# Second layer's first normalisation: gamma, beta and root applied by VectorE in two passes instead of by GpSimd in three

## The reference

```
# layer 2, end
out = out @ Wo + bo
x = out + hidden_state
mu = jnp.mean(x, axis=-1, keepdims=True)
var = jnp.var(x, axis=-1, keepdims=True)
return (x - mu) * jax.lax.rsqrt(var + EPS) * gamma + beta      # EPS 1e-06
# layer 3, begin
residual = hidden_states
x = layer_norm(hidden_states, ln1_w, ln1_b)                    # eps 1e-05
```

## Time and profile before

| | |
|---|---|
| time, median of 3 runs | 2528.74 us (2528.33 to 2530.09) |
| profiled execution | 2529.28 us |
| its span | 2527.1 us |
| TensorE busy | 2434.0 us, 96% |
| VectorE busy | 1253.2 us, 50% |
| GpSimd busy | 1119.7 us, 44% |
| ScalarE busy | 1096.3 us, 43% |
| mean granted clock of TensorE | 0.988 of 2.4 GHz |

### The profile page before, as it was taken

How to read it: one execution, slowest core, us unless ns; L and a number is a source line. 1 busy time by engine, 2 the same in 40 slices (tenths; PEclk the granted TensorE clock), 3 DMA queues, 4 the chain that set the end, 5 groups by cost and what they waited for, 6 DMA issues and landing times.

```text
span 2527.1 us, 49031 instructions
## 1 busy us (share of the span) xinstructions
PE 2434.0 (96%) x18400; PEld 2041.9 (81%) x18400; DVE 1253.2 (50%) x3744; ACT 1096.3 (43%) x3712; POOL 1119.7 (44%) x1972
## 2 busy tenths in 40 slices
PE   7999999999999999998888999999999999999999
PEld 6888887888888878886777788888888888788887
DVE  5665655323224667766787332233555565432332
ACT  5555654111114787787787111112555555211111
POOL 3444435600053787878797720042345433740000
PEclk9999999999999999998999999999999999999999
DMA  4121212311033223233353420022122111320100
GB/s 156 68 68 59 97 39 84 96 50 51 5 107 128 76 106 122 92 103 125 134 187 121 133 77 19 32 96 68 34 80 64 51 51 51 107 98 1 50 34 17
DMA packets 107866, 198.36 MB, mean 78 GB/s; under 512 B 9392, under 2 KB 36720, under 8 KB 104688
## 3 DMA queue, kind: packets, MB, share of 16 engines
q1 hardware_dynamic: 107632, 195.22, 23.0%
HBM read 136.47 MB, written 58.72 MB: 77 GB/s over the span
## 4 chain that ended last, share of the span: by engine, by line
PE 78%; ACT 9%; DVE 5%; POOL 4%; DMA 2%; issue 1%; SPq 0%; DVEq 0%; POOLq 0%
PE banks L327 69%; PE banks L468 5%; ACT plain_high L746 5%; PE banks L498 3%; ACT plain_low L746 2%; POOL plain_high L1404 2%; DVE plain_low L1034 1%; ACT plain_work L811 1%; POOL plain_low L1404 1%; DVE stats L1164 1%; PE banks L522 1%; ACT plain_work L730 1%; DVE rounded_low L1083 1%; DMA plain_high<-attention_w 0%; DVE plain_high L1034 0%
## 5 line engine op out<-in xcount | busy, mean ns | idle before, releaser
L327 PE MATMUL banks<-rounded_work,rounded_low 128*128 128x512 f32 (+1 forms) x2688 | 522.9, 349 | 11.7 <-DVE rounded_low L1202 9.1
L839 ACT ACTIVATE plain_work<-banks,columns 128x512 f32<-128x512 f32 x192 | 132.4, 690 | 860.9 <-PE banks L327 860.9
L327 PEld LDWEIGHTS banks<-rounded_work,rounded_low 128*128 128x128 f32 x2688 | 434.7, 193 | 76.2 <-issue 12.4
L327 PE MATMUL banks<-rounded_work,rounded_high 128*128 128x512 f32 (+1 forms) x2400 | 483.8, 355 | 1.4 <-DMA rounded_work<-ctx_split 0.9
L327 PEld LDWEIGHTS banks<-rounded_work,rounded_high 128*128 128x128 f32 x2400 | 397.0, 191 | 67.1 <-issue 5.5
L1373 DVE CAST rounded_work<-plain_work 128x512 fp32r<-128x512 f32 x192 | 104.5, 544 | 685.5 <-ACT plain_work L839 675.0
L1404 POOL TENSOR_SCALAR plain_high<-plain_high,inv_sum 128x128 f32<-128x128 f32 (+1 forms) x768 | 297.1, 413 | 303.5 <-DVE inv_sum L1056 303.1
L327 PE MATMUL banks<-rounded_low,rounded_work 128*128 128x512 f32 x1728 | 416.1, 392 | 0.0
L327 PE MATMUL banks<-rounded_high,rounded_work 128*128 128x512 f32 (+1 forms) x1728 | 391.4, 378 | 0.0
L327 PEld LDWEIGHTS banks<-rounded_low,rounded_work 128*128 128x128 f32 x1728 | 321.4, 188 | 70.6 <-issue 4.4
L327 PEld LDWEIGHTS banks<-rounded_high,rounded_work 128*128 128x128 f32 x1728 | 309.0, 188 | 62.5 <-issue 3.0
(11 more groups left out here) (109 smaller groups left out, 3327.9 us busy)
## 6 DMA issues: line engine op xcount, KB each, us to landing
plain_work<-x SPq DMA_DIRECT2D x96, 256.0 KB, 3.0
plain_work<-mlp_w SPq DMA_DIRECT2D x96, 256.0 KB, 2.7
rounded_work<-ctx_split SPq DMA_DIRECT2D x16, 1024.0 KB, 5.7
u<-plain_work SPq DMA_DIRECT2D x48, 256.0 KB, 2.1
plain_work<-u SPq DMA_DIRECT2D x12, 1024.0 KB, 7.1
x<-plain_work SPq DMA_DIRECT2D x48, 256.0 KB, 2.3
plain_work<-attention_w SPq DMA_DIRECT2D x44, 256.0 KB, 2.7
ctx_split<-rounded_work SPq DMA_DIRECT2D x8, 1024.0 KB, 5.6
```

The source lines that it names most:

```text
L327: mm = pe.matmul(dst, lhs(i), rhs(j), start=first and n == 0, stop=last and n == 2, skip_group_check=True)
L839: act.activation(gelu[:, j % 2, :], bank(key), ACT.Gelu_apprx_tanh, bias=col(m.y, 28 + j)).then_inc(evac_of(key), 1)
```

## The change

GpSimd keeps the first two steps of `pool_root` in the second layer, the epsilon and the power. The three passes behind them are dropped there. VectorE gets a new function `dve_unit`, called at the head of `dve_again`: it waits for GpSimd's root, computes (x - mean) * gamma in place in the hidden row, waits for that, and computes that times root plus beta, again in place. The second buffer is then written by `pool_again` alone, so the wait for its last store moves there. The first pass now raises the count `rooted` and the second raises `norm_ready`.

```
+        def dve_unit(dve, y, b):
+            rt = y.root(b)
+            i = rt % 2
+            h = hidden[:, b % 2, :]
+            if b == 0:
+                dve.wait_ge(gb_loaded, 32)
+            dve.wait_ge(rstd_done, rt + 1)
+            dve.scalar_tensor_tensor(out=h, in0=h, scalar=neg_mean[:, i:i + 1], in1=gamma, op0=ALU.add, op1=ALU.mult).then_inc(rooted, 1)
+            dve.wait_ge(rooted, rt + 1)
+            dve.scalar_tensor_tensor(out=h, in0=h, scalar=rstd[:, i:i + 1], in1=beta, op0=ALU.mult, op1=ALU.add).then_inc(norm_ready, 1)
```

```
@@ pool_root
-            u = (unit_g if y.kind == GQA else unit_c)[:, b % 2, :]
-            pool.wait_ge(u_stored[b % 2], stored_count(y.b0 + b - 2))
-            pool.tensor_scalar(u, h, neg_mean[:, i:i + 1], rstd[:, i:i + 1], ALU.add, ALU.mult).then_inc(rooted, 1)
-            if y.kind == GQA:
-                if b == 0:
-                    pool.wait_ge(gb_loaded, 32)
-                pool.wait_ge(rooted, rt + 1)
-                pool.tensor_tensor(u, u, gamma, ALU.mult).then_inc(scaled, 1)
-                pool.wait_ge(scaled, b + 1)
-                pool.tensor_tensor(h, u, beta, ALU.add).then_inc(norm_ready, 1)
@@ pool_again
+            pool.wait_ge(u_stored[b % 2], stored_count(y.b0 + b - 2))
```

More of the change, by code:

```diff
@@ L199, in build @@
         eps_done, rstd_done, rooted = sem("eps_done"), sem("rstd_done"), sem("rooted")
-        scaled, norm_ready = sem("scaled_by_gamma"), sem("norm_ready")
+        norm_ready = sem("norm_ready")
         u_stored = [sem(f"u_stored{i}") for i in range(2)]
@@ L1187, in dve_out @@
             dve_added(dve, y, b)
+        def dve_unit(dve, y, b):
[8 more added lines that the diff above has]
+            dve.scalar_tensor_tensor(out=h, in0=h, scalar=rstd[:, i:i + 1], in1=beta, op0=ALU.mult, op1=ALU.add).then_inc(norm_ready, 1)
         def dve_again(dve, y, b):
+            dve_unit(dve, y, b)
             dve.wait_ge(norm_ready, b + 1)
@@ L1428, in pool_root @@
                 pool.tensor_scalar(h, h, rstd[:, i:i + 1], 1.0, ALU.mult, ALU.mult).then_inc(rooted, 1)
-                return
-            u = (unit_g if y.kind == GQA else unit_c)[:, b % 2, :]
-            pool.wait_ge(u_stored[b % 2], stored_count(y.b0 + b - 2))
-            pool.tensor_scalar(u, h, neg_mean[:, i:i + 1], rstd[:, i:i + 1], ALU.add, ALU.mult).then_inc(rooted, 1)
-            if y.kind == GQA:
-                if b == 0:
-                    pool.wait_ge(gb_loaded, 32)
-                pool.wait_ge(rooted, rt + 1)
-                pool.tensor_tensor(u, u, gamma, ALU.mult).then_inc(scaled, 1)
-                pool.wait_ge(scaled, b + 1)
-                pool.tensor_tensor(h, u, beta, ALU.add).then_inc(norm_ready, 1)
+            elif y.kind == CROSS:
+                u = unit_c[:, b % 2, :]
+                pool.wait_ge(u_stored[b % 2], stored_count(y.b0 + b - 2))
+                pool.tensor_scalar(u, h, neg_mean[:, i:i + 1], rstd[:, i:i + 1], ALU.add, ALU.mult).then_inc(rooted, 1)
         def pool_again(pool, y, b):
```

## The result

The changed kernel takes 2565.39 us in the median of four runs, between 2556.7 and 2570.59; the kernel before took 2528.53 us beside it. The ratio is 1.0144, with a 95% interval of 1.0123 to 1.0165. It is slower, 36.9 us instead of the 24.9 us of the sum, and its runs lie 14 us apart where those of before lie 2.4 us apart. The profiled execution is the slowest of the four, 2570.59 us with a mean granted clock of 0.976; the fastest, 2556.7 us, had 0.981.

The account below looks back on a forecast made before the run. A closed loop over four engines was taken to bound each second-layer pair. Loop 17.2, first pairs 3.2, third layer 3.0 and clock 1.5 summed to 24.9 us on 2528.74, rounded to 2554 us; range 2541 to 2573.

Parts of the forecast that it names:

- The loop: Second layer's pairs: one closed loop over four engines; two passes cost 1.56 us a row, 17.2 us plus 3.2 us.
- TensorE's 96%: Rival for the whole kernel: TensorE's busy share is the bound and hides VectorE's additions; time stays at 2529 us; chance 0.05.
- the half-hidden case: Rival in the second layer's pairs: only one of the two places per pair is swallowed, giving 2541 us; chance 0.04.
- The wait: TensorE's wait for VectorE's query remainders in each pair grows from 0.85 us to about 2.4 us.
- The slack at TensorE's waits for GpSimd: In each pair, 0.51 + 0.76 = 1.27 us of clock loss is made up where TensorE waits for GpSimd.
- The clock: Second layer's pairs: TensorE's granted clock falls after the longer wait; 1.5 us taken, bounds 0 and 15 us.
- the clock decides: Rival: longer gaps drop TensorE's clock in nearly every pair beyond the slack; 2555 to 2567 us, counted above 2560; chance 0.18.
- GpSimd's relief at nothing: Removing GpSimd's passes, 53.5 us together, gains nothing in the loop, since its scaling waits for VectorE's reciprocal.
- The third layer: The last two rows fall into the third layer's first pair and cost 1.56 and 1.4 us, together 3.0 us.
- The port: Rival: each new VectorE pass stands until a GpSimd scaling ends; 35 us more, 2564 us; chance 0.13.

Follow-up runs that it names:

- the repeat: The changed kernel measured once more, unaltered: 2552.89 us (2551.74 to 2557.63), ratio 1.0107.
- even-rows kernel: The changed kernel with only the even rows getting VectorE's two passes, the odd ones keeping GpSimd's three: 2539.65 us, ratio 1.0051.
- odd-rows kernel: The changed kernel with only the odd rows getting VectorE's two passes, the even ones keeping GpSimd's three: 2549.77 us, ratio 1.0088.
- the filled kernel: The changed kernel plus 16 useless TensorE matmuls before round 2's first turn of probabilities in the second layer's pairs: 2554.26 us, ratio 1.0108.
- the kernel with GpSimd relieved: The kernel before, with GpSimd's three passes cut to 8 of 512 columns and VectorE unaltered: 2531.74 us, ratio 1.0015.

## Why the prediction was right, and where not

*The loop.* Right, at both places, for the reason given. The passes took 0.752 us each in the median (0.75 taken), a row 1.5 to 1.6 us from the first pass to the statistics (1.56 taken); the pair came to 50.47 us (50.4 forecast), and in the first pairs, where GpSimd's late scaling gives slack, to 47.69 + 2.79 = 50.48 without a long dip, in the repeat (47.69 + 2.63 forecast). TensorE's 96% did not hide anything, and the half-hidden case is out: the even-rows and the odd-rows kernel each pay.

*The wait.* Right: 2.38 us, 2.4 forecast. The slack at TensorE's waits for GpSimd is real too: in the pair with the short dip they shrank from 0.51 + 0.76 us to 0.49, and the pair lost nothing.

*The clock.* This is the term of the sum that was mis-sized: "I take half, 1.5 us; the bounds are 0 and, with two such losses per pair, 7 x (2 x 1.7 - 1.27) = 15 us." In the profiled execution the first four intervals lay 3.1, 3.2, 4.0 and 4.1 us above those of the filled kernel, 14.3 us together. The error was to take the loss of one dip at the end of the layer, 1.7 us, for the size of all of them. A dip here lasted 3.4 to 14 us. Short ones cost nothing; a long one cost 3.1 to 4.1 us, more than the 2.1 us that the upper bound allows a pair. That the total stayed below 15 us is luck: only four pairs had one. What the sum took as a value is a spread.

So the median of 2565.39 us lies in the range, but in the part above 2560 that the prediction gave to the rival *the clock decides* (0.18), not in the forecast from 2548 to 2560 (0.56); the sign named for that rival, pairs above 51.5 us with dips, was there in the first four. Without many long dips the forecast of 2554 us stands within 2 us of the filled and the repeated kernel (2554.26 and 2552.89). That it is so close is partly luck too, since two terms beside the clock were off in opposite directions, as the next two paragraphs say.

*GpSimd's relief at nothing.* Right in the loop, wrong by some 2 us once ahead of it: the first pass of the changed kernel starts at 864.2, where the statistics of that row started at 865.72 before, so this row's 1.56 us were not lost.

*The third layer.* 3.0 us were forecast; from the last interval's end to the layer's last moments it took 9.8 us longer, of which 1.5 us are the second layer's last row. The filled kernel took 7.2 us longer there, the even-rows kernel 2.3, the kernel with GpSimd relieved 4.7. Part of it is the clock again: in that stretch TensorE is busy 215.49 us instead of 211.28, at 0.91 instead of 0.93. The two rows' part cannot be read out of that; it stays open.

*The port.* No VectorE pass waited out a scaling: the longest took 0.859 us. GpSimd paid instead, and nobody waited for it:

```profile
986.13 3.63 POOL L1416 TENSOR_SCALAR plain_high<-plain_high,inv_sum 128x128 f32<-128x128 f32 x8 [0.21 <-DVE inv_sum L1056]
```

Eight scalings took 2.80 us at this place before. The rule of the Trainium skill (SBUF — State Buffer, Who interferes with whom), by which one of the two engines stands until the other's instruction ends, agrees with these runs in that they hold each other up. Here eight short GpSimd instructions lost 0.8 us together, and a VectorE pass at most 0.16 (0.859 against its shortest, 0.698). GpSimd's loss lay on the chain only where the passes stood between the reciprocals, in the first three pairs.

## What to carry to other kernels

A busy share of 96% on one engine does not make the other engines' work free: look for the closed loop through all engines, and price an addition by whether it stands ahead of or behind the wait on which its engine idles. The same two passes cost 27 us behind that wait (2552.89 against 2526.27 in the repeat) and 2.3 us ahead of its end (2524.36 against 2522.1). Where an addition lengthens a gap of TensorE, count what the granted clock does afterwards as a spread with a tail, not as a fixed price, and compare several runs.

## What was not expected

The same wait of 2.38 us led to dips of very different length, about 3.4 us (1098 to 1101) and about 14 us (989 to 1002), in one execution and behind the same instructions, and to none in a pair of the repeat. TensorE worked without a wait at the 1.2 GHz level in between, 4.00 of 4 us busy, and still was not raised. What decides that was not tried. Useless matmuls of 2.18 us a pair kept the 2.4 GHz level in the first five intervals and cost nothing: these are as long as a pair without a long dip, 50.5 us. The move of the second moments shortened the later pairs by 0.9 us instead of some 2 us and the first three by next to nothing, because ScalarE's or GpSimd's own list came next.
